# Attention's residual sum inside the projection's accumulation, and the low digit matched by one comparison with four candidates written by ScalarE

## What is computed

```python
h = _L0_tok_ref(x, kernel, bias)
h = h + _L0_attn_ref(_layernorm(h), Wq, bq, Wk, bk, Wo, bo, gamma, beta)
h = h + _L0_ffn_ref(_layernorm(h), Wq, bq, ln_g, ln_b, keys0, keys1, expert_down, expert_up)

# in the attention: the mean over three banded softmaxes, then
out = acc @ Wo + bo
res = x + out                       # x is the layer-normed input
return (res - mean(res)) * rsqrt(var(res) + EPS) * gamma + beta

# in the feed-forward part: for each of 8 heads, the best 16 of 64 scores on two key halves,
fi = take(ix0[..., :, None] + ix1[..., None, :], pos)    # 16 experts; fi is a sum of two indices, 0 to 126
out = einsum(gelu(x @ expert_down[fi]) * w, expert_up[fi])
```

## Time and profile before

| | us |
|---|---|
| median of 3 runs | 1349.89 (1349.42 to 1351.28) |
| the profiled execution, its own time | 1352.16 |
| its span, first to last instruction | 1350.4 |
| VectorE busy | 1243.1 (92%) |
| TensorE matmul, weight load | 995.4 (74%), 760.4 (56%) |
| GpSimd busy | 905.9 (67%) |
| ScalarE busy | 771.1 (57%) |
| DMA engines, mean over the span | about 5% |

### The profile page before, as it was taken

One profiled execution on the slowest core, in us unless ns is written; L12 is line 12 of the kernel. 1 busy time (PEld: TensorE's weight loads), 2 busy tenths in 40 slices (PEclk: granted clock), 3 DMA queues, 4 the chain that ended last, 5 costly groups with the idle time before them and its releaser, 6 DMA issues.

```text
span 1350.4 us, 38006 instructions
## 1 busy us (share of the span) xinstructions
PE 995.4 (74%) x10065; PEld 760.4 (56%) x10065; DVE 1243.1 (92%) x9664; ACT 771.1 (57%) x2115; POOL 905.9 (67%) x1926
## 2 busy tenths in 40 slices
PE   3855858778777786877878686877878777787644
PEld 2634646557556564765656475656747555564533
DVE  4339696999999999999999999999999999999995
ACT  2555747475574756657575665756566475745322
POOL 4338574767767677686767768676776867667551
PEclk7868877767788787767878787777768788776655
DMA  2020000000000000000000000000000000000000
GB/s 51 7 34 9 9 13 9 14 10 6 13 13 13 10 16 10 7 13 13 14 10 9 17 6 13 10 17 9 7 20 6 14 4 17 4 6 15 6 7 7
DMA packets 36073, 16.53 MB, mean 12 GB/s; under 512 B 15792, under 2 KB 35648, under 8 KB 35858
## 3 DMA queue, kind: packets, MB, share of 16 engines
q1 hardware_dynamic: 35234, 13.82, 4.2%
q10 hardware_dynamic: 624, 0.30, 0.1%
HBM read 7.59 MB, written 6.01 MB: 10 GB/s over the span
## 4 chain that ended last, share of the span: by engine, by line
DVE 63%; issue 11%; POOL 9%; PE 7%; ACT 6%; SPq 2%; DMA 0%; DVEq 0%; POOLq 0%; ACTq 0%
DVE idx L1593 17%; DVE val L1591 12%; DVE scores L1596 9%; DVE cr L1664 7%; DVE oh L1606 5%; DVE best L1662 4%; DVE wl L1626 2%; POOL qscale L679 2%; DVE masked L1546 2%; DVE bns L1516 2%; PE banks L1222 1%; PE bankM L1344 1%; ACT act_g L939 1%; DVE prod L1635 1%; ACT probs L887 1%
## 5 line engine op out<-in xcount | busy, mean ns | idle before, releaser
L1593 DVE FIND_INDEX8 idx<-val,scores 128x8 uint16<-128x64 f32 x1472 | 292.1, 217 | 0.0
L1591 DVE MAX8 val<-scores 128x8 f32<-128x64 f32 x1472 | 201.7, 208 | 0.0
L1344 PE MATMUL bankM<-wl,oh 128*128 128x16 f16 x5888 | 160.6, 172 | 29.3 <-DVE wl L1626 23.9
L1344 PEld LDWEIGHTS bankM<-wl,oh 128*128 128x128 f16 x5888 | 161.5, 101 | 32.0 <-DVE wl L1626 25.9
L679 POOL TENSOR_TENSOR qscale<-nmx,power 128x16 f32<-128x16 f32 x46 | 137.5, 2990 | 52.7 <-DVE nmx L1570 52.7
L1596 DVE MATCH_REPLACE8 scores<-val,scores 128x64 f32<-128x64 f32 x736 | 145.4, 208 | 0.0
L1606 DVE TENSOR_SCALAR oh<-eh 128x1024 f16<-128x1024 int16 x368 | 133.0, 429 | 3.1 <-ACT eh L1023 3.1
L1307 PE MATMUL bankS<-wgk,hnT 128*128 128x512 f32 x184 | 127.2, 781 | 0.0
L1352 PE MATMUL bankM<-up_x,prod 128*128 128x128 f32 x368 | 80.9, 390 | 46.4 <-DVE prod L1635 46.3
L1023 ACT ACTIVATE eh<-bankM,digit_bias 128x256 int16<-128x256 f32 x184 | 72.7, 489 | 69.1 <-PE bankM L1329 69.1
L1222 PEld LDWEIGHTS banks<-diag,probs 124*124 124x124 f32 x672 | 106.1, 243 | 9.4 <-issue 6.8
(11 more groups left out here) (204 smaller groups left out, 2866.6 us busy)
## 6 DMA issues: line engine op xcount, KB each, us to landing
h_in<-h_rows SPq DMA_DIRECT2D x45, 64.0 KB, 2.6
out<-o_sb SPq DMA_DIRECT2D x45, 64.0 KB, 1.5
x_in<-in_x SPq DMA_DIRECT2D x16, 93.8 KB
x_in<-in_x SPq DMA_DIRECT2D x16, 62.5 KB
h_rows<-hsum SPq DMA_DIRECT2D x16, 62.0 KB
h_rows<-hsum SPq DMA_DIRECT2D x16, 61.0 KB
h_rows<-hsum SPq DMA_DIRECT2D x16, 60.5 KB
x_in<-in_x SPq DMA_DIRECT2D x16, 31.0 KB
```

Source lines behind the costliest of these rows:

```text
L1344: last = e.matmul(coef[:, g, :, :], oh[:, k, g, :, :].rearrange("p v t -> p (v t)"), wl[:, part, k, :, TG * g:TG * (g + 1)], start=k + par ...
L1591: last = v.max(out=v_[:, hd, s, best8], in_=src[:, hd, s, :])
L1593: last = v.max_index(out=i_[:, hd, s, best8], in_max=v_[:, hd, s, best8], in_values=src[:, hd, s, :])
```

## The change

TensorE now adds `xb` into the projection: behind each row tile's matmul with `wo_sb` (now `stop=False`) comes a second one of the identity and `xb[:, t, :]` into the same place. Ahead of the first row tile's matmul it waits for `xb_ready`. `p1_res` is gone; `res` is now the name of the place in PSUM, `bn_stats` and `p1_ln` read it there, and `wo_done` takes the place of `res_ready`. Nothing else moves in any engine's order.

In `one_low` the mask of two bits is gone, and with it VectorE's wait for it. ScalarE writes, behind the four `eh` copies and a wait for them, four int16 candidates `low_same[l] = 4 * eh[0] + l`, before it copies `expert` and `wm`. VectorE compares `expert` with the four in one instruction of the same shape. `low_same` is complete before `expert` counts `high_ready`, on which `one_low` waits. The constants `lows` (VectorE) give way to four `low_bias` columns set by GpSimd at the start.

```diff
--- before.py
+++ after.py
@@ -171,7 +171,6 @@
         diag = sb("diag", [NT, 3, NT])
         attnT = sb("attnT", [NT, 3 * NT])
         axT = sb("axT", [D, NT])
-        res = sb("res", [NT, 3, D])
         xh = sb("xh", [NT, 3, D])
         h = [sb(f"hsum{p}", [NT, 3, D]) for p in range(2)]
         hn = sb("hn", [NT, 3, D])
@@ -213,10 +212,10 @@
         wm = sb("wm", [128, 2, 2, QT], f16)
         eh = sb("eh", [128, SHIFTS, 2, QT], i16)
         expert = sb("expert", [128, 2, QT], i16)
-        el = sb("el", [128, 2, QT], i16)
         oh = sb("oh", [128, 2, NG, EH, TG], f16)
         ol = sb("ol", [128, 2, EL, QT], f16)
-        lows = sb("lows", [128, EL, QT], i16)
+        low_same = sb("low_same", [128, 2, EL, QT], i16)
+        low_bias = sb("low_bias", [128, EL])
         wl = sb("wl", [128, 2, 2, EL, QT], f16)
         prod = sb("prod", [128, EL, QT])
         o_sb = sb("o_sb", [QT, 3, D])
@@ -233,6 +232,7 @@
         bankS = ctx.enter_context(nc.psum_tensor("bankS", [128, 1024], f32))
         bankM = ctx.enter_context(nc.psum_tensor("bankM", [128, 1024], f32))
         q_sums_ps = bankQ[0:QT, 0:10 * PAIRS].rearrange("p (k c) -> p k c", c=10)
+        res = bankC[0:NT, D:4 * D].rearrange("p (t d) -> p t d", d=D)
         wcT_ps = bankS[0:2 * NC, :].bitcast(f16).rearrange("p (k n) -> p k n", k=2)
         merged = bankM[:, :].rearrange("p (k n) -> p k n", k=2)
         coef = bankM[:, 0:NG * EL * TG].rearrange("p (g l t) -> p g l t", g=NG, l=EL)
@@ -279,7 +279,6 @@
         ax_done = sem("ax_done")
         axT_ready = sem("axT_ready")
         wo_done = sem("wo_done")
-        res_ready = sem("res_ready")
         xh_ready = sem("xh_ready")
         h_ready = sem("h_ready")
         hn_ready = sem("hn_ready")
@@ -316,7 +315,6 @@
         merge_done = sem("merge_done")
         wm_ready = sem("wm_ready")
         high_ready = sem("high_ready")
-        digits_ready = sem("digits_ready")
         onehigh_ready = sem("onehigh_ready")
         wl_ready = sem("wl_ready")
         scattered = sem("scattered")
@@ -576,6 +574,8 @@
                 g.memset(guard8[:, :], 1.0e-24)
                 g.memset(std3[:, H + 1:32], 0.0)
                 g.memset(std3[:, H:H + 1], 1.0)
+                for l in range(EL):
+                    g.memset(low_bias[:, l:l + 1], float(l))
                 for j in range(SHIFTS):
                     last = g.memset(digit_bias[:, j:j + 1], -(EL - 1) / 2.0 / EL - VALUES * j)
                 last.then_inc(setup_pool, 1)
@@ -631,7 +631,7 @@
             def p1_xb(c):
                 b = c.b
                 pool.wait_ge(xl_ready, b + 1)
-                wait(pool, res_ready, b)
+                wait(pool, wo_done, 3 * b)
                 g.tensor_tensor(xb[:, :, :], xl[:, :, :], bob.unsqueeze(1).to_broadcast([NT, 3, D]), ALU.add).then_inc(xb_ready, 1)
 
             def p1_h(c):
@@ -1018,10 +1018,12 @@
                 act.wait_ge(merge_done, n + 1)
                 wait(act, wl_ready, 2 * n)
                 wait(act, onehigh_ready, 2 * n)
-                wait(act, digits_ready, n)
                 for j in range(SHIFTS):
                     last = a.activation(eh[:, j, :, :], merged[:, :, 2 * QT:3 * QT], ACT.Identity, bias=digit_bias[:, j:j + 1], scale=1.0 / EL)
                 last.then_inc(high_ready, 1)
+                act.wait_ge(high_ready, 2 * n + 1)
+                for l in range(EL):
+                    a.activation(low_same[:, :, l, :], eh[:, 0, :, :], ACT.Identity, bias=low_bias[:, l:l + 1], scale=float(EL))
                 a.activation(expert[:, :, :], merged[:, :, 2 * QT:3 * QT], ACT.Copy).then_inc(high_ready, 1)
                 a.activation(wm[:, :, :, :].rearrange("p k s n -> p k (s n)"), merged[:, :, 0:2 * QT], ACT.Copy).then_inc(wm_ready, 1)
 
@@ -1238,7 +1240,11 @@
             def p1_wo(c, t):
                 b, n = c.b, c.tile(t)
                 pe.wait_ge(axT_ready, n + 1)
-                e.matmul(bankC[0:NT, (1 + t) * D:(2 + t) * D], axT[:, :], wo_sb[:, :], start=True, stop=True).then_inc(wo_done, 1)
+                if t == 0:
+                    pe.wait_ge(xb_ready, c.b + 1)
+                out_t = bankC[0:NT, (1 + t) * D:(2 + t) * D]
+                e.matmul(out_t, axT[:, :], wo_sb[:, :], start=True, stop=False)
+                e.matmul(out_t, id32[0:NT, 0:NT], xb[:, t, :], start=False, stop=True).then_inc(wo_done, 1)
 
             def p1_turn_hn(c):
                 b = c.b
@@ -1431,8 +1437,6 @@
                     for w in range(3):
                         last = v.memset(probs[t][w][:, :], 0.0)
                 v.memset(bias_in, 0.0)
-                for l in range(EL):
-                    v.memset(lows[:, l, :], l)
                 v.memset(key_z[:, :, :], 0.0).then_inc(zeroed, 1)
 
             setup_link = linker(dve, setup_dve, 13, 0)
@@ -1509,7 +1513,7 @@
                 if i == 0:
                     dve.wait_ge(h0_ready, 2 * (b + 1))
                 elif i == 1:
-                    dve.wait_ge(res_ready, b + 1)
+                    dve.wait_ge(wo_done, 3 * (b + 1))
                 else:
                     dve.wait_ge(h_ready, 3 * (b + 1))
                 for t in range(3):
@@ -1552,14 +1556,6 @@
                 dve.wait_ge(probs_ready, n + 1)
                 wait(dve, diag_ready, n)
                 v.reciprocal(rden[:, :], den[:, :]).then_inc(rden_ready, 1)
-
-            def p1_res(c):
-                b = c.b
-                dve.wait_ge(wo_done, 3 * (b + 1))
-                dve.wait_ge(xb_ready, b + 1)
-                wait(dve, xh_ready, b)
-                v.tensor_tensor(res[:, :, :].rearrange("p t d -> p (t d)"), bankC[0:NT, D:4 * D],
-                                xb[:, :, :].rearrange("p t d -> p (t d)"), ALU.add).then_inc(res_ready, 1)
 
             def q_guard(c, t):
 
@@ -1610,12 +1606,8 @@
             def one_low(c, t):
                 m = c.flat(t)
                 dve.wait_ge(high_ready, 2 * (m + 1))
-                v.tensor_scalar(el[:, :, :], expert[:, :, :], EL - 1, None, ALU.bitwise_and).then_inc(digits_ready, 1)
-                dve.wait_ge(digits_ready, m + 1)
-                if isinstance(m, int) and m == 0:
-                    dve.wait_ge(zeroed, 2)
-                v.tensor_tensor(ol[:, :, :, :], el[:, :, :].unsqueeze(2).to_broadcast([128, 2, EL, QT]),
-                                lows[:, :, :].unsqueeze(1).to_broadcast([128, 2, EL, QT]), ALU.is_equal).then_inc(wl_ready, 1)
+                v.tensor_tensor(ol[:, :, :, :], expert[:, :, :].unsqueeze(2).to_broadcast([128, 2, EL, QT]), low_same[:, :, :, :], ALU.is_equal)\
+                 .then_inc(wl_ready, 1)
 
             def low_weights(c, t):
                 m = c.flat(t)
@@ -1776,7 +1768,6 @@
                 each(low_weights, c + -1, 2)
                 each(rank, c, 1, 0, 0)
                 do(p1_wsq, c + 2)
-                do(p1_res, c + 1)
 
 
             run(dve, start, body, lambda: None)
```

## The result

The change makes the kernel slower. The median of the kernel after is 1370.28 us (1369.68 to 1372.25) against 1350.59 us of the kernel before on the same chip (1349.42 to 1351.73), a ratio of 1.0147 with a 95% interval of 1.0131 to 1.0163. That is about 20 us. Forecast were 1352.8 us, with a range to 1363: the result lies outside it. The profiled execution of the kernel after has a span of 1370.4 us, that of before had 1350.4.

A forecast was written before the change was run, and what follows sets the result against it. VectorE was taken to bound the kernel: 16.5 us saved less 13.5 of waits gains 3.0; with 4.4 for the start and 1.5 for smaller parts, +2.9 us gives 1352.8 us, range 1342 to 1363.

The forecast's parts named there:

- What bounds the kernel: VectorE, busy 92% of the span: whatever leaves its queue shortens the run, unless a wait comes in its place.
- The sum: `res` leaving VectorE saves 0.46 us in each of 16 batches, 7.4 us, 6.0 of it behind 250 us.
- The bound that rested on the Trainium skill's page: `bn_stats` reading PSUM: 62 cycles more each would give back 48 x 65 ns, 3.1 us; the forecast took no cost.
- The mask: `el` leaving VectorE in `one_low` saves 0.25 us at each of 46 tiles, 11.5 us, 10.5 behind 250 us.
- The candidates: ScalarE's four `low_same` copies take 0.40 us each; with 0.15 for the wait, `expert` comes 1.75 us late.
- The margins: `expert` lies ready 1.11, 1.54 or 2.27 us before `one_low`; these margins don't grow, so the delay costs 13.5 us.
- The start: Four tiles before 250 us pay 5.9 us for ScalarE's delay; three sums give back 1.5: a cost of 4.4 us.
- The smaller parts: TensorE's added matmuls, its wait for `xb` and ScalarE's slip behind tile 1 cost 1.5 us, bounds 0 and 9.
- the second rival: The delay travels through TensorE after tile 1 until `finish` waits: 8 us more, 1361 us; chance 0.21.
- the three rivals: Margins hold, 1339.5 us (0.24); delay travels through TensorE, 1361 us (0.21); comparison `ol` gets slower, 1375 us (0.03).
- a long wait of `o_sb` or `prod`: VectorE waiting long at `o_sb` or `prod` would show the delay travelling through TensorE, 1361 us; chance 0.21.
- another time of `ol`: `ol` taking another time than 692 ns would show a slower comparison: at 1.1 us, 22 us more, 1375; chance 0.03.

The follow-up runs named there:

- The half alone: Kernel before with only the attention's sum moved to TensorE, the low digit as before: 1345.13 us, ratio 0.9954.
- the digit's half: Kernel before with only the low digit changed to ScalarE's four candidates, `res` still on VectorE: 1369.62 us, ratio 1.0127.
- the gap: Kernel after, VectorE waiting for its own `ol` at tile 2: 1364.68 us, ratio 1.0102; the same with candidates as constants: 1334.89 us, 0.9877.
- the early guard: Kernel after with `q_guard` (`nmx`) of tile 1 ahead of the last choose step: 1360.21 us, ratio 1.0060; with candidates as constants too: 1335.32 us, 0.9890.
- the three kernels with the power let in: Kernel after with a wait ahead of `nmx`, a wait behind `ol`, or `q_guard` moved earlier: 1364.34, 1364.68 and 1360.21 us.
- with constants: Kernel after with candidates written once at the start instead of ScalarE's four copies, low digit left out: 1340.22 us, ratio 0.9919.
- A gap ahead of `nmx`: Kernel after with VectorE waiting for its own two one-hot instructions ahead of `nmx` of tile 1: 1364.34 us, ratio 1.0101.

## Why the prediction was wrong

**What bounds the kernel** was read rightly: a thousand microseconds of VectorE without a stop, and a loss as soon as waits came. Its condition, "unless a wait comes in its place", is what came true. **The sum** (-7.4 us): right alone, wrong in the changed kernel. The half alone gives 6.2, and `bns` from PSUM takes 288 ns against 279, which makes 0.2 us over the stretch; beside the digit's half it gives nothing, since waits take its place. The bound that rested on the Trainium skill's page "VectorE: DVE Perf Modes", section "The TRN2 errata — SBUF-src ops pay a fixed extra latency per instruction", an estimate of 65 ns for each, is not borne out: 9 ns. **The mask** (-11.5 us): right in VectorE's own time, 8.5 us of instructions and 1.4 of gaps in 39 tiles, 0.25 for each. In all the saving measured 16.6 us with the gap and 14.9 with the early guard, where the sum had 18 (16.5 and 1.5). **The candidates** (0.40 us each, `expert` 1.75 late): right; 0.40, and 3.57 against 1.85, so 1.72. `ol`'s 692 ns: right.

**The margins** (13.5 us of waits for `expert`): the waits grew by 13.5 us, 1.0 to 14.5. That this equals the forecast is partly luck, since it has two causes. With the power let in early they are 8.7 to 9.5 us in three kernels, against 12.7 to 14.5 in three with the stretched power, so some 5 us of them go with it. The likely way is GpSimd's work ahead of the merge; it was not traced. The margins of tile 0 show the effect: taken as the time from the end of `expert`, less the 1.72 us of delay, to the moment when VectorE is ready for it, their mean over the stretch is 1.13 us in the kernel before, 0.83 in the kernel after, and 1.21 to 1.27 in the three kernels with the power let in. The step "these margins don't grow with the change" holds in its words, but its reason, that VectorE's work in between stays as it is, left out GpSimd, and the margins of tile 0 shrank. **The start** (4.4 us; its parts as printed add to 6.0 less 1.5, not 5.9): 4.8, right as far as one pair of executions can tell.

**The smaller parts** (1.5 us, bounds 0 and 9) are the first of two terms that failed. The text followed ScalarE's lateness behind tile 1 through the sums of squares and TensorE's queue as far as `smax`, and for the second rival as far as `finish`. It did not follow it to GpSimd. One place of the kernel after, on TensorE, ScalarE, GpSimd and VectorE:

```profile
483.60 3.84 PE L1224 MATMUL banks<-diag,probs 124*124 124x124 f32 x18
487.27 0.30 PE L1300 MATMUL bankQ<-q_lin,hnT 128*128 128x16 f32 x2
...
487.85 0.19 ACT L969 ACTIVATE half_sums<-bankQ 128x32 f32<-128x32 f32 x1
...
488.12 0.22 POOL L671 TENSOR_TENSOR nlin<-half_sums,std 128x16 f32<-128x16 f32 x1 [3.04 <-ACT half_sums L969]
...
490.25 0.24 POOL L711 TENSOR_TENSOR cs<-val_s 128x32 f32<-128x32 f32 x1
...
490.64 0.55 DVE L1654 MAX8 best<-cs 128x8 f32<-128x50 f32 x4 [2.16 <-POOL cs L711]
```

GpSimd waits 3.04 us for `half_sums`, which waits for a matmul queued on TensorE behind 3.84 us of the attention's turning. Its `cs` stands behind `nlin` in GpSimd's queue, and `best` waits 2.16 us. Such waits are 8.6 us in the kernel after and 6.5 to 13.6 in the three kernels that let the power in. The same delay of ScalarE cost 23 us on the kernel before, 23 in the changed one with the early guard and 30 in it with the gap; the prediction's 20.9 us (13.5, 5.9 and 1.5) was near the first two. Where the 7 us between them come from stays open. This is the second rival's mechanism, a delay that travels through TensorE, with another end than `finish`.

**The term that stood nowhere** is GpSimd's power. No step asked what the removed instruction had done for another engine. `el` was followed by a wait of VectorE for itself, a gap of 35 ns, and GpSimd used it. The kernel after against the one with the gap put back: 1.0147 - 1.0102, 6 us, a difference good to about 3, and the same in two kernels with such a gap. Against the one with the early guard, which also lets the power start earlier, it is 11.8 us.

How the miss of 17 us splits depends on the kernels that one goes through. By the gap behind `ol`: 1.4 us of saving (18 less 16.6), 9.5 of delay (30.4 less 20.9) and 6.1 of the power. By the early guard: 3.1, 2.1 and 11.8. Each is good to about 3. That either list comes to 17.0 proves nothing: the three are differences along one chain of kernels from before to after, and add up by construction. What both ways share is that the power, which the forecast had at nothing, costs some 6 to 12 us, and that without it the kernel would still have been slower than forecast, at 1360 to 1365 us. Two of the three rivals' signs, a long wait of `o_sb` or `prod` and another time of `ol`, were absent, rightly.

Two things stay open. A gap ahead of `nmx` let the power in as well, although the power only came 0.16 us into `ol`; the trace doesn't show why a gap that is over by then still helps. And the further 4 to 6 us that the early guard brings in the kernel after (1360.2 against 1364.7 us), but not with constants (1335.3 against 1334.9), were not followed to their place; they are the same 7 us by which the two prices of the copies differ.

## What to carry to other kernels

An instruction that is removed from the busiest engine takes its waits with it, and a gap of a few tens of ns may be what lets another engine in: look, for each gap that closes, at what runs beside it on GpSimd. When an engine is made late, follow its results through every queue to the next meeting with the bound engine, not only through the first. A margin measured in the old kernel is made of the work that stands in it, and two small losses, each covered alone, can use it up together. So measure the halves of a change apart and together: here a half that gained 6.2 us alone gained nothing beside the other.

## What the hardware showed that was not expected

- A GpSimd power of 128x16 takes 2.91 to 2.92 us at tile 1 of the kernel before, begun 0.09 us ahead of `ol`. Begun 0.16 us into `ol`, it takes 3.30 where a gap of 35 ns follows or stands shortly before, and 5.84 where VectorE runs `ol`, four `oh` and two `wl` (3.1 us) without a gap. The Trainium skill, "SBUF — State Buffer", section "Who interferes with whom", has an exclusive lock between the two engines; by its section "SBUF: two separate sides" whichever starts first holds it for its whole instruction. The rows agree that one keeps the other out; they differ in the length, since the power stayed out over seven VectorE instructions and not over one. They differ in who is kept out, too: the power of tile 0 in the kernels with constants began 0.5 to 0.6 us ahead of eight `oh` and an `ol` without a gap, and took 4.00 us, to 0.05 us behind the last of them, in place of 2.91.
- It works in the other direction as well: two `oh` of 0.42 us took 1.17 each beside GpSimd operations of 128x400.
- The same with a small VectorE instruction: `lnm`, 124x3 elements, takes 0.64, 0.72 or 0.81 us in the rows above, with the same operands, and each time ends 0.01 to 0.02 us behind the GpSimd operation of 128x400 beside it (494.98 and 494.96, 493.07 and 493.05, 506.25 and 506.24). Such an instruction is shown as long, not as waiting. In the kernel before, all 28 `lnm` that start beside such an operation end so, and 19 of the 20 others take 0.15 to 0.16 us.
- ScalarE reads PSUM no slower here: `xh` took 454 ns from PSUM and 482 from SBUF.
